# A convolution over 2x2 pixel blocks, attention products issued in halves, and a new order of work, in a fused convolution, attention and expert kernel

## The chip, the cores and the metric

The kernel runs on one core of a Trainium2 chip. The time is that of the device, in microseconds (us), as a median of runs; one further execution was taken with the hardware profiler. A core has a tensor engine (PE; PEld is its loading of weights), a vector engine (DVE), a scalar engine (ACT), GpSimd (POOL), SP, which here only issues transfers, and 16 DMA engines. Each works through its own list of instructions in order and waits on semaphores. Results of PE land in PSUM, eight banks of 512 float32 columns.

## The reference

The input x is float32, 32 batches of 128 channels and 32x32 pixels. Per batch:

```python
xn   = layernorm over channels(x)                    # weights ln_w, ln_b
bcdt = w_bcdt (64x128) @ xn                          # 64 channels
bcdt = conv3x3(bcdt, w_gw, 32 groups of 2 channels, padding 1)
BC, dt = first 32 channels, last 32 channels         # 1024 pixels each
AB   = softmax(dt + A, over pixels) * BC
h    = x @ AB.T                                      # 128 x 32
x    = w_out @ (h @ BC) + x
```

Then, over the 1024 tokens (pixels) of a batch, with t the token rows: one attention layer on the normalised rows (q, k of 64 channels, v of 128, all with a leaky relu, softmax over 1024 keys, residual, layernorm with gamma and beta), added to t. Last, an expert layer over all 32768 tokens: a gate picks one of 8 experts, each token takes the next place of its expert in the order of tokens up to a capacity of 5120, the expert's two matrices (128 to 512 with relu, 512 to 128) are applied, the result is scaled by the gate's probability and added. The output has the layout of x.

## The kernel before, in words

Two programs follow each other. `token_program` (lines 68 to 1259) does everything up to the gate and scatters the normalised-row data of each token into its expert's slots in DRAM, and the token rows themselves (`tokens`) as well. `finish_program` (from line 1263) runs the experts over 71 blocks of 512 slots, scatters the results into `tokens`, and turns finished batches back to channels by pixels.

The work of a batch is cut into named steps ("x_turn", "xs", "bcdt", "bT_turn", "conv", "dt", "dt_exp", "cd_turn", "h", "hh", "g", "y", "ts", "u1n", "u1_turn", "qk", "qk_lrelu", "qk_high", "qk_low", "v", "mask", "mx", "negmax", "mrow", "st", "pv", "ln2s", "ln2n", "ln2m", "ln2g", "t1b", "rowid", "ln3s", "u2_turn", "gate", "gate_turn", "pos", "scatter"). Each engine has a function `one(st, ...)` with its own part of a step, and all engines walk the same list of steps, written out by hand: `head` (line 243), then `steps` (line 222) 20 times, one pass for each new batch, then `tail`. A pass works on five batches at once: its entries carry an offset, so that the convolution of batch c+2, the scores of c+1 and c and the gate of c-1 stand interleaved. An engine that is ready early waits for the semaphore of its step; nothing is reordered at run time.

What the change touches, by step:

- x: SP loads a batch with one transfer (line 439), 4 KB for each channel, issued at "x_turn" of the batch before; "x_turn" on PE transposes it in eight pieces to pixels by channels (even pixels, then odd, line 1098), ACT copies all 1024 columns (two banks, `work`) at once.
- "bcdt": eight products of 64 columns; DVE multiplies by 1/std; "bT_turn" transposes so that the 128 partitions hold 64 channels at even columns and 64 at odd columns of the image; ACT adds a bias and writes the padded image `img` (lines 708, 710).
- "conv" (line 1128): six products of 512 columns, for two column shifts and three rows, into one bank. "dt": DVE takes the maximum over 512 pixels (line 890), exchanges it between the two pixel halves, forms the shift of the exponential (lines 892 to 898); ACT copies BC and exponentiates dt (lines 716, 719).
- "cd_turn": one small product sums exp(dt) over the pixel halves (line 1135), four transposes. "h": eight products of 32 columns of weights, summing into four column groups. "hh" (line 1149): one product with `ident2` that adds the four groups. "g" (1154): with w_out; DVE scales by the softmax's sum (916). "y" (1159): eight products of 128 columns, over 32 rows each, in two banks; DVE adds x (921).
- attention: "mx" (1085) computes the scores for the maxima, DVE reduces them (858); "negmax" and "mrow" turn four rows of maxima, and SP copies them into the last row of `qhi` (489); "st" (1194, 1196) computes the scores again as two products, the second with that row, and ACT exponentiates to `pT`. "pv" (1222): for each of 8 groups of 128 queries, eight products of 129 columns, which alternate between two banks; DVE divides and adds (971, 973).
- "t1b" (GpSimd, line 620) fills the token rows of the next stage once the scatter of two batches before has landed; DVE's sum of "y" waits for the "t1b" of the batch before.
- "pos" (1249 to 1254): eleven small bfloat16 products that count, for each token, the earlier tokens of its expert.
- expert stage: `turn_out` (1594) transposes finished rows and `evict` (1403) writes them to every second column of the output tile, even pixels and odd pixels in turn.

## Time and profile before

| | us |
|---|---|
| median of 3 runs | 2141.65 (2141.04 to 2142.93) |
| profiled execution, its own time | 2142.42 |
| its span, first to last instruction | 2140.7 |
| busy in it: PE, PEld | 2003.1, 1642.3 |
| busy in it: DVE, ACT, POOL | 1753.5, 1192.6, 1023.7 |
| token stage, last PE work of it | about 1570 |
| expert stage, first PE work of it | 1590.87 |

A group of the profile is a set of like instructions; "busy" is the time in which at least one of them ran, so with overlapping instructions count times mean is more than busy. A float32 matmul of the program shows as two instructions. An idle time is put down to whatever ended it.

### The profile page before, as it was taken

The numbers are of one execution on the slowest core, as the hardware profiler recorded it, in microseconds if no ns is written. First come the engines' busy times: TensorE is split into PE (matmuls) and PEld (weight loads), VectorE is DVE, ScalarE is ACT, GpSimd is POOL, SyncE is SP. The second block draws the span as 40 slices with busy tenths as digits, with TensorE's granted clock in tenths as the row PEclk, the third lists the DMA queues.
The fourth block names the chain that finished last, engine by engine and source line by source line (L and its number), as shares of the span: only waits on it lengthen the run. The fifth ranks groups of instructions, "written<-read, shape, count | busy, mean of one in ns | idle before, by whom it ended". The sixth has DMA issues, their size and how long they took to land. (4 is left out here: it accounts for less than half of the span.)

```text
span 2140.7 us, 41957 instructions
## 1 busy us (share of the span) xinstructions
PE 2003.1 (94%) x13855; PEld 1642.3 (77%) x13855; DVE 1753.5 (82%) x5467; ACT 1192.6 (56%) x2216; POOL 1023.7 (48%) x1243
## 2 busy tenths in 40 slices
PE   5889999999999999999999999999829999999996
PEld 3567777787778787778787777787629999898985
DVE  3568888888888888888888888888739999898985
ACT  2344555555555555555545555545327777777773
POOL 5112544444544444544444544354436765555654
PEclk7799999999999999999999999999959999999997
DMA  4541323222312111212111212111136778788874
GB/s 179 193 151 35 93 67 95 70 66 60 88 53 70 51 51 52 77 53 70 51 51 55 75 52 69 49 41 47 44 108 197 205 227 268 251 261 261 253 244 174
DMA packets 163512, 243.98 MB, mean 114 GB/s; under 512 B 31039, under 2 KB 110478, under 8 KB 163296
## 3 DMA queue, kind: packets, MB, share of 16 engines
q1 hardware_dynamic: 139856, 187.16, 29.5%
q0 software_dynamic: 17280, 31.84, 4.6%
q10 hardware_dynamic: 6160, 22.30, 2.6%
q8 instruction: 111, 1.82, 0.4%
q14 instruction: 105, 0.86, 0.1%
HBM read 115.95 MB, written 95.56 MB: 99 GB/s over the span
## 5 line engine op out<-in xcount | busy, mean ns | idle before, releaser
L1222 PE MATMUL pvp<-va,pT 128*128 128x129 f32 x4096 | 505.3, 276 | 0.2 <-ACT pT L747 0.2
L1222 PEld LDWEIGHTS pvp<-va,pT 128*128 128x128 f32 x4096 | 485.5, 191 | 22.2 <-issue 12.4
L1393 POOL DMA_INDIRECT token_rows<-res x284 | 313.0, 1102 | 221.2 <-DVE res L1526 148.3
L858 DVE TENSOR_REDUCE mxs<-mxp 128x1 f32<-128x512 f32 x512 | 338.6, 680 | 23.7 <-PE mxp L1085 17.9
L747 ACT ACTIVATE pT<-stp 128x512 f32<-128x512 f32 x512 | 288.5, 597 | 105.8 <-PE stp L1196 101.1
L639 POOL DMA_INDIRECT expert_slots<-rows,slot_i x256 | 284.7, 1112 | 100.7 <-issue 89.3
L1579 PEld LDWEIGHTS e_yp<-w2s,hid 128*128 128x128 f32 x2272 | 294.1, 192 | 19.8 <-ACT hid L1456 0.3
L1579 PE MATMUL e_yp<-w2s,hid 128*128 128x128 f32 x2272 | 299.8, 275 | 0.0
L1456 ACT ACTIVATE hid<-e_hp,b1c 128x512 f32<-128x512 f32 x284 | 195.1, 687 | 112.9 <-PE e_hp L1571 104.9
L1194 PE MATMUL stp<-qhl,klh 128*128 128x512 f32 x512 | 238.7, 466 | 1.3 <-ACT pT L747 0.8
L1085 PE MATMUL mxp<-khi,qhi 127*128 127x512 f32 x512 | 220.5, 459 | 11.7 <-issue 6.4
L1196 PE MATMUL stp<-qhi,khi 128*128 128x512 f32 x512 | 203.4, 397 | 0.0
L1128 PE MATMUL work<-img,wtap 128*128 128x512 f32 x384 | 174.4, 604 | 2.5 <-ACT img L710 2.5
L708 ACT ACTIVATE img<-work,cbias 64x512 f32<-64x512 f32 x32 | 21.8, 682 | 229.2 <-PE work L1119 229.2
L1569 PE MATMUL e_hp<-e_up,w1p 128*128 128x512 f32 x284 | 136.3, 480 | 2.4 <-DVE e_up L1499 2.4
L679 ACT ACTIVATE u<-t,shift_t,rstd_t 128x128 f32<-128x128 f32 x256 | 105.1, 482 | 59.0 <-POOL shift_t L591 59.0
L679 ACT ACTIVATE o<-o,shift,rstd 128x128 f32<-128x128 f32 x256 | 105.2, 483 | 57.1 <-POOL shift L591 56.4
L1128 PEld LDWEIGHTS work<-img,wtap 128*128 128x128 f32 x384 | 71.8, 194 | 83.1 <-issue 81.2
L1427 ACT ACTIVATE e_u<-e_rows 128x128 f32<-128x128 f32 x284 | 123.4, 485 | 21.6 <-DMA e_rows<-expert_slots 21.6
L1085 PEld LDWEIGHTS mxp<-khi,qhi 127*128 127x128 f32 x512 | 93.5, 192 | 51.3 <-DVE mxs L858 30.1
L586 POOL TENSOR_SCALAR var_x<-mv_x 128x8 f32<-128x8 f32 x32 | 8.0, 250 | 242.3 <-DVE mv_x L851 242.3
L1194 PEld LDWEIGHTS stp<-qhl,klh 128*128 128x128 f32 x512 | 97.6, 191 | 32.0 <-issue 16.0
(242 smaller groups left out, 3919.8 us busy)
## 6 DMA issues: line engine op xcount, KB each, us to landing
w1p<-w_parts SPq DMA_DIRECT2D x71, 512.0 KB
expert_slots<-fill ACTq DMA_DIRECT2D x32, 660.0 KB, 4.2
e_rows<-expert_slots SPq DMA_DIRECT2D x71, 264.0 KB, 3.2
w2s<-in_w SPq DMA_DIRECT2D x71, 256.0 KB
xs<-in_x SPq DMA_DIRECT2D x32, 512.0 KB, 5.0
token_rows<-rows SPq DMA_DIRECT2D x32, 512.0 KB, 3.8
f_rows<-token_rows SPq DMA_DIRECT2D x32, 512.0 KB, 6.5
out<-f_cols SPq DMA_DIRECT2D x32, 512.0 KB, 7.3
```

What stands on the lines that cost most here:

```text
L639: g.indirect_dma_start(out=slots, out_offset=bass.IndirectOffsetOnAxis(ap=slot_i[k][:, t:t + 1], axis=0), in_=rows[k][:, t, :], in_offset= ...
L679: last = a.activation(dst[:, t, :], src[:, t, 0:C], ACT.Identity, bias=shift_[:, t:t + 1], scale=rstd_[:, t:t + 1])
L747: a.activation(pT[j][:, kt, :], stp[kt % 2][:], ACT.Exp).then_inc(s["exp_ready"], 1)
L858: v.reduce_max(mxs[:, qt, n % 2:n % 2 + 1], mxp[n % 2][:], AX).then_inc(s["mx_read"], 1)
L1085: mm(mxp[n % 2][:], qhi[k][0:TOP, qt * P:(qt + 1) * P], khi[k][0:TOP, (n % 2) * HALF:(n % 2 + 1) * HALF], start=True, stop=True).then_inc( ...
L1128: last = mm(work[:, 0, :], wtap[:, d, kh, :], img[:, kh:kh + H, d:d + W // 2], start=(d == 0 and kh == 0), stop=(d == 1 and kh == 2))
L1194: mm(stp[kt % 2][:], klh[k][:, kt * P:(kt + 1) * P], qhl[k][:, c * HALF:(c + 1) * HALF], start=True, stop=False)
L1196: mm(stp[kt % 2][:], khi[k][:, kt * P:(kt + 1) * P], qhi[k][:, c * HALF:(c + 1) * HALF], start=False, stop=True).then_inc(s["st_done"], 1)
L1222: last = mm(pvp[qt % 2][:, 0:VA], pT[c][:, kt, n * P:(n + 1) * P], va[k][:, kt, :], start=(kt == 0), stop=(kt == NT - 1))
L1393: g.indirect_dma_start(out=tokens, out_offset=bass.IndirectOffsetOnAxis(ap=res[n % 2][:, q, TOKEN:TOKEN + 1].bitcast(I32), axis=0), in_=re ...
L1456: a.activation(hid[f][:], hp[f][:], ACT.Relu, bias=b1c[n % WBUF][:, f:f + 1], scale=1.0)\
L1579: last = mm(yp[n % 2][:, q, :], hid[f][:, q * P:(q + 1) * P], w2s[n % WBUF][:, f, :], start=(f == 0 and q == 0), stop=(f == FC - 1), skip_ ...
```

## The change

- Pixels of a batch are split in two ways, by row parity and by column parity. x is loaded by row parity: two transfers for each batch, each of every second image row (32 pixels, 128 bytes). Token order follows: a group of 128 tokens holds one row parity and one column parity, and the products of "pos" and the output writes are rearranged for it.
- The 64 channels of bcdt stand as two halves of 32 (BC and dt). The 128 partitions of the image hold 4 pixel positions of a 2x2 block by 32 channels of one half. The convolution is eight products of 256 columns: for each half, four block shifts.
- The bias of the layernorm is no longer added to the image: the image's border is set to its negative once, and the convolution of the bias is added at the copies of BC and dt.
- "dt" exchanges its maxima over four groups of partitions, two exchanges instead of one. "hh" is one product with `same_s` (128 columns), "g" has 128 columns of weights; its scaling moves from DVE to ACT, as four instructions. "y" is four products of 256 columns over 64 rows.
- ACT's and DVE's evictions of the two banks of `work` (x, u1, qk, u2, v) are done bank by bank, each when its bank is ready.
- "pv" is split: "pv_first" issues the first four of its eight products, "pv" the other four and the rest.
- `steps`, `head` and `tail` have a new order. The first batch's waits and constants change with it.

```diff
-        steps = [(("mrow", 1), 0), ("t1b", 0), ("mask", 1), ("conv", 2), ("qk_high", 1), ("qk_low", 1),
-                 (("ln2n", 3), -1), ("dt", 2), ("dt_exp", 2), (("st", 1, 0), 0), (("st", 1, 1), 0), ("ln2m", -1),
...
-                 (("st", 1, 7), 0), ("y", 2), (("pv", 1, 0), 0), (("mrow", 0), 1), ("ts", 2), ("u2_turn", -1),
-                 (("pv", 1, 1), 0), ("gate", -1), ("ln3s", -1), (("pv", 1, 2), 0), (("u1n", 0), 2), (("u1n", 1), 2),
-                 (("u1n", 2), 2), (("mx", 1, 0), 1), (("pv", 1, 3), 0), (("st", 0, 0), 1), (("u1n", 3), 2),
...
-                 ("pos", -1), (("mx", 1, 5), 1), ("v", 2), (("pv", 0, 0), 1), (("mx", 1, 6), 1), ("bcdt", 3),
-                 ("ln2s", 0), (("mx", 1, 7), 1), (("negmax", 1), 1), ("scatter", -1), (("pv", 0, 1), 1),
...
+        steps = [("t1b", 0), ("qk_lrelu", 1), (("pv", 0, 2), 0), (("mrow", 1), 0), ("mask", 1), ("qk_high", 1),
+                 ("ln2m", -1), ("conv", 2), (("pv_first", 0, 3), 0), ("dt", 2), (("st", 1, 0), 0), ("dt_exp", 2),
+                 (("mx", 0, 0), 1), ("ln2g", -1), (("st", 1, 1), 0), (("mx", 0, 1), 1), (("st", 1, 2), 0),
...
+                 ("qk_low", 1), (("pv", 0, 3), 0), (("mx", 0, 6), 1), (("mx", 0, 7), 1), (("st", 1, 7), 0), ("y", 2),
+                 (("negmax", 0), 1), ("ln3s", -1), (("pv_first", 1, 0), 0), (("pv_first", 1, 1), 0), (("mrow", 0), 1),
+                 ("u2_turn", -1), (("pv", 1, 0), 0), ("ts", 2), (("pv", 1, 1), 0), ("gate", -1), ("x_turn", 3),
+                 (("st", 0, 0), 1), ("gate_turn", -1), (("pv_first", 1, 2), 0), (("st", 0, 1), 1), (("st", 0, 2), 1),
...
+                 ("u1_turn", 2), (("st", 0, 6), 1), ("xs", 3), ("scatter", -1), (("st", 0, 7), 1), (("mx", 1, 3), 1),
...
-                sp.dma_start(xs[k][:], x[bass.ds(b, 1)].rearrange("o c n -> (o c) n")).then_inc(x_loaded[k], 16)
+                for r in range(2):
+                    sp.dma_start(xs[k][:, r * HALF:(r + 1) * HALF].rearrange("c (m w) -> c m w", w=W),
+                                 x[bass.ds(b, 1)].rearrange("o c (m r w) -> (o c) r m w", r=2, w=W)[:, r]).then_inc(x_loaded[k], 16)
...
-                    a.activation(img[0:U, 1:H + 1, 0:W // 2], work[0:U, 1, :].rearrange("p (h w) -> p h w", h=H),
-                                 ACT.Identity, bias=cbias[0:U, :], scale=1.0)
-                    a.activation(img[U:P, 1:H + 1, 1:WP], work[U:P, 1, :].rearrange("p (h w) -> p h w", h=H),
-                                 ACT.Identity, bias=cbias[U:P, :], scale=1.0).then_inc(s["img_ready"], 1)
+                    im = work[:, 1, :].rearrange("p (a r q) -> p a r q", a=2, q=W // 2)
+                    for e in range(2):
+                        for r in range(2):
+                            own = slice((2 * e + r) * S, (2 * e + r + 1) * S)
+                            last = a.copy(img[own, :, r:r + H // 2, e:e + W // 2], im[own])
+                    last.then_inc(s["img_ready"], 1)
...
+                if st == "g":
+                    act.wait_ge(s["g_done"], b + 1)
+                    act.wait_ge(s["dt_sumr"], b + 1)
...
+                    for g in range(Q4):
+                        own = slice(g * S, (g + 1) * S)
+                        last = a.activation(gs[own, g % 2, :], work[own, 0, 0:C], ACT.Identity, scale=dtr[own, :])
+                    last.then_inc(s["g_ready"], 1)
...
-                    v.reduce_max(dts[U:P, 0:1], work[U:P, 0, :], AX).then_inc(s["dt_small"], 1)
+                    v.reduce_max(dts[:, 0:1], work[:, 1, 0:NQ], AX).then_inc(s["dt_small"], 1)
...
+                    v.tensor_tensor(dts[:, 2:3], dts[:, 0:1], dts[:, 1:2], ALU.max).then_inc(s["dt_small"], 1)
+                    dve.wait_ge(s["dt_small"], b * 6 + 3)
+                    for g in range(Q4):
+                        last = v.tensor_copy(dts[g * S:(g + 1) * S, 3:4], dts[(g ^ 1) * S:((g ^ 1) + 1) * S, 2:3])
...
-                    for d in range(2):
-                        for kh in range(3):
-                            last = mm(work[:, 0, :], wtap[:, d, kh, :], img[:, kh:kh + H, d:d + W // 2],
-                                      start=(d == 0 and kh == 0), stop=(d == 1 and kh == 2))
+                    for h in range(2):
+                        for d in range(4):
+                            dr, dq = d // 2, d % 2
+                            last = mm(work[:, h, 0:NQ], wtap[:, h, d, :], img[:, h, dr:dr + H // 2, dq:dq + W // 2],
+                                      start=(d == 0), stop=(d == 3))
...
-                        pe.wait_ge(s["state_ready"], 1)
+                        pe.wait_ge(s["mask_ready"], 1)
...
-                    mm(work[:, 0, 128:128 + 2 * S], hT[:], ident2[:], start=True, stop=True).then_inc(s["h_done"], 1)
+                    mm(work[:, 0, P:2 * P], hT[:], same_s[:], start=True, stop=True).then_inc(s["h_done"], 1)
...
-                    for jj in range(Q4):
+                    for j in range(2):
                         for e in range(2):
-                            last = mm(work[:, e, jj * P:(jj + 1) * P], cd[e * S:(e + 1) * S, jj * P:(jj + 1) * P],
-                                      gs[e * S:(e + 1) * S, :], start=True, stop=True)
+                            last = mm(work[:, e, j * 2 * P:(j + 1) * 2 * P], cd[e * U:(e + 1) * U, 0, j * P:(j + 1) * P],
+                                      gs[e * U:(e + 1) * U, :, :].rearrange("p r c -> p (r c)"), start=True, stop=True)
...
+                if isinstance(st, tuple) and st[0] == "pv_first":
...
+                    for kt in range(NT // 2):
+                        mm(pvp[qt % 2][:, 0:VA], pT[c][:, kt, n * P:(n + 1) * P], va[k][:, kt, :],
+                           start=(kt == 0), stop=False)
...
-            copy(cols[b % 2][:].rearrange("c (m e) -> c e m", e=2)[:, e, :], bank(x)[:])\
+            copy(cols[b % 2][:].rearrange("c (m p q e) -> c e p m q", p=2, q=W // 2, e=2)[:, e],
+                 bank(x)[:].rearrange("c (p m q) -> c p m q", p=2, q=W // 2))\
```

## Rows read from the trace of the kernel before

**Rows 1.** The page, parts 1 and 2: busy us (share), and PE's granted clock.
```profile
PE 2003.1 (94%) x13855; PEld 1642.3 (77%) x13855; DVE 1753.5 (82%) x5467; ACT 1192.6 (56%) x2216; POOL 1023.7 (48%) x1243
...
PEclk7799999999999999999999999999959999999997
```
**Rows 2.** Windows: us, each engine's busy (instructions), clock, DMA share, GB/s.
```profile
600.00:1400.00 800.00, 788.40 (x5558) 627.32 (x5558) 686.32 (x2476) 433.46 (x803) 370.34 (x487) 1.00 0.21 58
...
1640.00:1800.00 160.00, 159.65 (x1138) 147.15 (x1138) 148.25 (x280) 124.72 (x234) 103.47 (x93) 1.00 0.75 228
```
**Rows 3.** Timeline of PE in the loop: start, us, instruction.
```profile
1001.76 0.33 PE L1149 MATMUL work<-ident,hT 128*128 128x64 f32 x2
...
1004.75 1.16 PE L1159 MATMUL work<-gs,cd 32*128 32x128 f32 x16
...
1024.54 0.23 PE L1249 MATMUL pvp<-oh_bf,before_bf 128*128 128x64 bf16 x2
...
1024.84 0.48 PE L1085 MATMUL mxp<-khi,qhi 127*128 127x512 f32 x1
...
1035.31 5.32 PE L1128 MATMUL work<-img,wtap 128*128 128x512 f32 x12
...
1040.69 0.39 PE L1196 MATMUL stp<-qhi,khi 128*128 128x512 f32 x1
...
1047.52 0.33 PE L1149 MATMUL work<-ident,hT 128*128 128x64 f32 x2
```
**Rows 4.** Groups by line and shape, PE, 600 to 1400 us: busy, mean ns, idle before.
```profile
L1128 PE MATMUL work<-img,wtap 128*128 128x512 f32 x204 | 90.4, 592 | 0.0
...
L1159 PE MATMUL work<-gs,cd 32*128 32x128 f32 x272 | 19.7, 283 | 0.0
```
**Rows 5.** Waits, 600 to 1400 us: who waited for whom: us, times, longest.
```profile
DVE t L921 <- POOL rows L620: 15.3, 16, 1.3
PEld mxp L1085 <- DVE mxs L858: 13.3, 50, 0.5
...
PE work L1069 <- DVE t L921: 7.3, 16, 0.8
```
**Rows 6.** Groups by line and shape, DVE and ACT, 600 to 1400 us.
```profile
L890 DVE TENSOR_REDUCE dts<-work 64x1 f32<-64x512 f32 x17 | 11.8, 694 | 29.3 <-PE work L1128 29.3
...
L916 DVE TENSOR_SCALAR gs<-work,dtr 64x128 f32<-64x128 f32 x17 | 5.8, 342 | 2.2
...
L892 DVE COPY dts<-dts 32x1 f32<-32x1 f32 x17 | 2.5, 148 | 0.6
...
L679 ACT ACTIVATE u<-t,shift_t,rstd_t 128x128 f32<-128x128 f32 x144 | 59.1, 482 | 26.6 <-POOL shift_t L591 26.6
...
L710 ACT ACTIVATE img<-work,cbias 64x512 f32<-64x512 f32 x17 | 11.6, 684 | 0.2
...
L725 ACT COPY exT<-work 128x256 f32<-128x256 f32 x17 | 6.3, 372 | 8.3 <-PE work L1137 8.3
```
**Rows 7.** DMA packets from 4 to 6 us, then from 1010 to 1016 us.
```profile
DMA packets 1253, 0.23 MB, mean 117 GB/s; under 512 B 1112, under 2 KB 1240, under 8 KB 1253
...
DMA packets 1193, 1.06 MB, mean 176 GB/s; under 512 B 36, under 2 KB 1064, under 8 KB 1192
```
**Rows 8.** Timeline of the start: start, us, instruction, idle before it.
```profile
6.78 0.87 DVE L817 TENSOR_SCALAR wln<-wbc,lnw_c 128x64 f32<-128x64 f32 x1 [6.78 <-DMA gw_s<-in_gate_w]
...
30.73 0.24 PE L1135 MATMUL work<-dts,pairs 64*64 64x1 f32 x2 [2.54 <-ACT cd L719]
...
31.51 0.10 POOL L581 MEMSET reach<- 128x1 f32 x1
```
**Rows 9.** Timeline in the loop; last, a transfer's size and us to landing.
```profile
1008.96 0.66 SPq L489 DMA_DIRECT2D qhi<-nt  x1
...
1015.61 0.48 PE L1194 MATMUL stp<-qhl,klh 128*128 128x512 f32 x1
...
token_rows<-rows SPq DMA_DIRECT2D x17, 512.0 KB, 3.8
```

More of the change, by code:

```diff
@@ L18 @@
 S = 32
-HP, WP = H + 2, W // 2 + 1
+HB, WB = H // 2 + 1, W // 2 + 1
+NQ = N // 4
 Q4 = 4
@@ L531, in _ @@
             pool.wait_ge(s["early_ready"], 1)
-            chain(g.memset(pairs[:], 0.0))
-            for d in (U - S, U, U + S):
-                chain(g.affine_select(out=pairs[:], in_=pairs[:], pattern=[[-1, U]], compare_op=ALU.not_equal, fill=1.0,
-                                      base=-d, channel_multiplier=1))
             chain(g.memset(fill[:], 0.0))
@@ L748, in one @@
                 if st == "u2_turn":
-                    act.wait_ge(s["u2_turned"], b + 1)
                     if not first:
                         act.wait_ge(s["gate_done"], b)
-                    a.copy(u2T[:], workf).then_inc(s["u2T_ready"], 1)
+                    for h in range(2):
+                        act.wait_ge(s["u2_turned"], b * 2 + (h + 1))
+                        last = a.copy(u2T[:, h * HALF:(h + 1) * HALF], work[:, h, :])
+                    last.then_inc(s["u2T_ready"], 1)
                 if st == "gate":
@@ L1054, in _ @@
             mm(mxp[0][:, 192:192 + E], mean_m[:], gw_s[:], start=True, stop=True)
-            mm(mxp[0][:, 128:129], wbc[:].rearrange("p a u -> p (a u)"), lnb_c[:], start=True, stop=True)\
-                .then_inc(s["wcen_psum"], 1)
+            for h in range(2):
+                last = mm(mxp[0][:, 128 + h:129 + h], wrep[:, h, :, :].rearrange("c a u -> c (a u)"), lnb_c[:], start=True, stop=True)
+            last.then_inc(s["wcen_psum"], 1)
             def taps():
@@ L1132, in one @@
                     if first:
-                        pe.wait_ge(s["state_ready"], 1)
+                        pe.wait_ge(s["mask_ready"], 1)
                     wait_apart(pe, s["cd_exp"], b + 1, passed["pe"])
-                    mm(work[0:U, 0, 256:257], pairs[U:P, :], dts[U:P, 4:5], start=True, stop=True).then_inc(s["dt_sum"], 1)
-                    for jj in range(Q4):
-                        last = nc.tensor.transpose(work[:, 1, jj * P:(jj + 1) * P], cd[:, jj * P:(jj + 1) * P], ident[:])
+                    mm(work[:, 0, 256:257], same_s[:], dts[:, 4:5], start=True, stop=True).then_inc(s["dt_sum"], 1)
+                    for n in range(4):
+                        last = nc.tensor.transpose(work[:, 1, n * P:(n + 1) * P], cd[:, n // 2, n % 2 * P:(n % 2 + 1) * P], ident[:])
                     last.then_inc(s["cd_turned"], 1)
@@ L1169, in one @@
                     for h in range(2):
-                        last = mm(work[:, h, :], wqk_s[:], u1T[:, h * HALF:(h + 1) * HALF], start=True, stop=True)
-                    last.then_inc(s["qk_done"], 1)
+                        mm(work[:, h, :], wqk_s[:], u1T[:, h * HALF:(h + 1) * HALF], start=True, stop=True).then_inc(s["qk_done"], 1)
                 if st == "mask":
@@ L1257, in one @@
+                    for g in range(Q4):
+                        mm(pg[:, 1:3], ones_bf[:], oht[:, :, g:g + 1, :].to_broadcast([P, 2, Q4, E]),
+                           start=False, stop=False, skip_group_check=True)
+                    for g in range(Q4):
+                        last = mm(pg[:, 2], ones_bf[:], oht[:, 0, g:g + 1, :].to_broadcast([P, Q4, E]),
+                                  start=False, stop=(g == Q4 - 1), skip_group_check=True)
                     last.then_inc(s["pos_done"], 1)
```

333 lines of the change are left out of this document (196 added, 137 removed), and 331 rows, old and new, of tables (head, steps, tail).

## The prediction

> **What bounds the kernel now.** I read the page's first two parts first: TensorE (PE) is busy 94% of the span, and the granted clock is full except at the start, at one dip and at the end [rows 1]. The busy time by stage then shows two different kernels. In the token stage (600 to 1400 us) PE is busy 788.40 of 800 us and VectorE (DVE) 686.32, with the DMA engines at 21%; in the expert stage (from 1640) PE is busy 159.65 of 160 [rows 2]. The change touches the token stage and, in the expert stage, only the order in which finished rows are turned and written. So its worth is read in the token stage.
>
> One pass of the token loop can be timed by one matmul that occurs once in it: the product "hh" starts at 1001.76 and again at 1047.52, so a pass is 45.76 us [rows 3]. There are 32 batches; I treat each as costing one pass, head and tail included. PE is idle 11.6 us in these 800, 0.66 a pass. With so little idle, matmul time that goes is time that goes, as long as VectorE (39.3 us of work a pass) and the waits don't take its place.
>
> **The change, part by part.**
>
> *The convolution.* Before, six matmuls of 512 columns, each run by the chip as two instructions: 204 instructions in 17 passes, 90.4 us [rows 4], 5.32 us a pass. The timeline agrees: started at 1035.31, and the second half of the next score pair, which can't start before the first has streamed, at 1040.69 [rows 3]; 5.1 to 5.3 us. After, eight matmuls of 256 columns: 16 instructions instead of 12, with half the columns each. By columns that is 4096 against 6144, 2/3, or 3.55 us: -1.77. Bounds: if an instruction had a price of its own beside its columns, the gain shrinks; with all of the price fixed it would be 16/12 x 5.32 = 7.09, +1.77. What speaks against that end is the y row: instructions of 128 columns cost 19.7/272 = 0.07 us each [rows 4], far below 0.44, so the price goes with the columns. I take -1.7; from -1.8 to -1.3.
>
> *y.* Sixteen instructions with 128 columns, two row groups of 32, 1.16 us [rows 3]. After: eight with 256 columns, two row groups of 64, into the same two banks. If neighbours overlap as now, the same; if the pairs stop overlapping, eight times the 0.22 us of a 256-column instruction (0.443/2) is 1.8, +0.6. I take 0; -0.2 to +0.6.
>
> *hh, g and the sum over dt* use 128 instead of 64 columns or rows: no row has these shapes; from nothing to twice the y instruction's 0.07 each, six instructions: 0 to +0.4; I take +0.15. *The placing product (pos)* goes from 11 instructions to 15: from 1024.54 to 1024.84 is 0.30 us for 11 [rows 3], so +0.1 (0 to +0.2).
>
> Matmul time in sum: -1.7 + 0 + 0.15 + 0.1 = -1.45 a pass, 32 times: **-46 us**.
>
> *The stall at the turning of u2.* The waits show one chain that ends on PE: VectorE's sum t waits for GpSimd's rows (15.3 us in 16 waits), which waits for the scatter's DMA, and then PE waits for t, 7.3 us in 16 waits [rows 5]. In the new list the scatter stands 21 entries before the next "t1b" instead of 9, so the rows are there in time. What is late next is "y" itself, whose sum needs its matmuls and g's longer scaling before them. 0.42 us a pass in about 26 passes: **-11 us** (0 to -15, or a new stall of any size, below).
>
> *VectorE.* The maximum over dt reads 256 columns instead of 512: of 694 ns about half, -0.35. The scaling of g leaves for ScalarE, -0.34. Five more instructions of one column at about 150 ns are added in the dt chain, +0.75, one larger copy +0.07, the split of vz +0.15 [rows 6]. Net +0.3: 39.6 us in a pass of 44. Its idle time falls from 6.4 to 4.7 a pass. PE's weight loads for the maximum products already wait for it 13.3 us in 17 passes [rows 5], 0.76 a pass; if that grows as the idle time shrinks, by 6.4/4.7, it is +0.27, in 27 passes about **+7 us** (0 to +20).
>
> *ScalarE (ACT)*, 433.46 us in 17.5 passes [rows 2]. Two image writes of 684 ns become four of the same length, +1.0 (or four of the plain copy); g's scaling becomes four instructions between 372 and 482 ns, +1.7; halved evictions cost about 0.15 each, four times; cd and exp are halved, -0.4 [rows 6]. About +2.9 on 24.8 us a pass: 28 of 44. It is not the bound, but g's step has become 1.7 us where it was 0.34, and the image 2.4 for 1.37. In the loop other products lie between in the list and hide that; in the first and the last batch nothing does: +2.3 each, less 0.5 for each halved eviction: **+3 us**. That cover gone in the loop would cost up to 2.3 a pass.
>
> *Loads of x.* One transfer of 128 long runs becomes two that pick every second image row, 128 bytes a run: 4096 packets. Around 4 to 6 us the queues moved 1253 mostly short packets in 2 us; from 1010 to 1016 they moved 1193, mostly of 512 bytes, in 6 us, not always busy [rows 7]. So 6.5 us from the nearer row, at most 20.6. In the loop this lies beside a pass of 44 us, and in the list the next transfer on SP's queue ("mrow" of the other half) comes half a pass later, some 22 us, so it costs nothing; with that cover gone, up to 20 us a pass. At the start it is exposed: the first weights, queued behind x, end VectorE's idle 6.78 us [rows 8]. I take +3 us (0 to +14).
> The Trainium skill, DMA: Bandwidth & Descriptors, section Specifications, asks for at least 512 B a transfer for line rate; the two rows agree only in that the short packets moved fewer bytes (0.23 MB in 2 us against 1.06 in 6), and by it alone the load would be slower in each batch, still hidden, and the sum unchanged but for the start.
>
> *Constants.* The first "cd_turn" now waits for the last of GpSimd's constants, which ended at 31.6, with two masks more some 32.3; before, its first matmul ran at 30.73 [rows 8]. So it is 1.5 us later, and the first batch's convolution saves nothing (+1.7): **+3 us**, beside the +3 of x.
>
> *Evictions in the expert stage, products in two halves.* The same instructions with other strides, and the same 16 matmuls with others between: 0. The first half of a product cannot start before the same waits as the whole, so splitting only gives PE something to do while a bank is being freed; that is in the stall term.
>
> **Sum**, against the profiled execution's own 2142.42 us (2140.7 of span and 1.7 around it): -46 - 11 + 7 + 3 + 3 + 3 = -41, so 2101; the median of the runs shown is 0.8 lower than that execution, so I forecast **2100 us**, 1.9% faster.
>
> **Rivals.**
> *A, the new row of maxima arrives late (slower).* Of the first half, today the transfer is issued at 1008.96 and the score product that needs it starts at 1015.61, 6.6 us later [rows 9]. In the new list there lie between "mrow" and that product only the turn of u2, two half products, the gate and the turn of x: 8 x 0.11 + 2 x 0.9 + 0.6 + 0.9 = 4.2 us after the transpose, some 3 after the issue. And the stores of token rows (3.8 us to landing [rows 9]) and of the low parts now stand ahead of it in the same queue, where they stood behind it. If the transfer needs 3.8 us as the store does and starts after it, the product waits 0.8 to 4.6 us a pass. At the middle, 2.7 us in 27 passes, it is +73: 2173. It decides from 41/27 = 1.5 us a pass. For it: the order of the list. Against it: the store is ready once t2 is, half a pass earlier; only the low parts hold SP back, and about 5 us of matmuls lie between them and "mrow".
> *B, the new order removes more.* A pass has more in it than its columns: PE's idle, the wait on VectorE and gaps at changes of shape. If another 0.8 a pass goes, -25: 2075. For it: the halves and the evictions by bank shorten each hand-over. Against: only 0.66 a pass is idle.
> *C, half of the gain is eaten*: y without overlap (+0.6 a pass) or VectorE as the new bound near 45 us: +20, so 2120.
> The Trainium skill, TensorEngine Tiling (Array Packing), section Key Properties, says that a change of tiling mode drains TensorE; y goes from four row tiles' mode to two's, h keeps its own, so the number of changes stays, and no row here prices one.
> *D, it does not do what it says*: if a matmul instruction of 256 columns cost what one of 512 does, +1.77 instead of -1.7 a pass, +110, 2210. The y row speaks against it.
>
> **How the numbers follow.** Forecast 0.50 (2085 to 2112), B 0.15 (2060 to 2085), C 0.19 (2112 to 2138), A 0.14 (of which 0.03 near no change), D 0.02. Range 2065 to 2140: it leaves out half of B's lower tail, and A and D, about 0.2. A measurement of this kernel tells about 0.2% from no change, 4.3 us. Faster 0.84, same 0.03, slower 0.13.
>
> **What would show it.** The convolution at about 213 ns of busy time for each of 16 instructions; a pass of 44.2 us between two hh; no wait of PE for t; VectorE near 90% in the loop; the first weights landed at about 10 instead of 6.8 us; expert stage from its first row to its last unchanged. Wrong: score products of the first half waiting at the head of PE for the maxima's transfer; a pass above 45; y at 1.8 us.

## The result, and the profile after

The changed kernel takes 2055.49 us (median of 4 runs, 2051.71 to 2057.47) against 2142.17 (2141.04 to 2142.93) of the kernel before on the same chip: ratio 0.9594, 95% interval 0.9577 to 0.9610. That is 86.7 us faster. The forecast was 2100 with a range from 2065; the time lies below the range, and below the band of the fastest rival, B (2060 to 2085). Its profiled execution took 2056.32 us, with a span of 2054.6.

The page of the changed kernel, parts 1 and 2, and its window over the loop (columns as in [rows 1, 2]):

```profile
PE 1934.3 (94%) x13873; PEld 1669.8 (81%) x13873; DVE 1744.1 (85%) x5637; ACT 1274.3 (62%) x2550; POOL 1042.5 (51%) x1242
...
PEclk8799999999999999999999999999779999999997
```
```profile
600.00:1400.00 800.00, 794.34 (x5885) 676.48 (x5884) 723.88 (x2715) 504.32 (x1036) 414.33 (x519) 1.00 0.27 62
```

PE's share of the span is 94% as before: that number says nothing of the gain. What moved is PEld, from 627.32 to 676.48 us of 800 [rows 2], and VectorE, from 686.32 to 723.88. More work fits in a stretch, since a pass became shorter: of weight loads a pass has 36.4 us, where it had 35.9. The timeline of PE in the loop answers [rows 3]:

```profile
993.02 0.42 PE L1226 MATMUL work<-same_s,hT 128*128 128x128 f32 x2
...
1010.15 0.23 PE L1337 MATMUL pvp<-oh_bf,before_bf 128*128 128x64 bf16 x2
...
1010.56 0.48 PE L1271 MATMUL stp<-qhl,klh 128*128 128x512 f32 x1
...
1025.85 3.73 PE L1205 MATMUL work<-img,wtap 128*128 128x256 f32 x16
...
1035.89 0.46 PE L1226 MATMUL work<-same_s,hT 128*128 128x128 f32 x2
...
1039.03 1.13 PE L1236 MATMUL work<-gs,cd 64*128 64x256 f32 x8
```

From hh to hh it is 42.87 us, where it was 45.76. Over the whole kernel, by the starts of the hh products: the first came at 39.9 us (34.0 before, +5.9); from the first to the last, 31 passes, it is 1344.9 us (1429.7, -84.8); from the last to the first product of the expert stage 121.1 (127.2, -6.1); from there to the end 548.7 (549.8, -1.1). In sum -86.1, the difference of the spans.

The groups of the loop that answer to [rows 4, 6] (busy, mean ns | idle before):

```profile
L1205 PE MATMUL work<-img,wtap 128*128 128x256 f32 x288 | 66.9, 384 | 0.0
L1236 PE MATMUL work<-gs,cd 64*128 64x256 f32 x152 | 21.6, 402 | 0.2 <-ACT gs L781 0.2
L757 ACT COPY img<-work 32x512 f32<-32x512 f32 x72 | 41.7, 579 | 103.0 <-PE work L1190 102.4
L781 ACT ACTIVATE gs<-work,dtr 32x128 f32<-32x128 f32 x76 | 27.0, 355 | 2.9 <-PE work L1231 2.1
L959 DVE COPY dts<-dts 32x1 f32<-32x1 f32 x76 | 11.0, 145 | 1.4
L946 DVE TENSOR_REDUCE dts<-work 128x1 f32<-128x256 f32 x19 | 8.0, 423 | 4.6 <-PE work L1205 4.6
```

The convolution is 66.9/288 = 232 ns an instruction, 3.7 us a pass instead of 5.3 (forecast: 213 ns and 3.55). y is 21.6/19 = 1.14 us, as before (1.16). So these two terms of the forecast hold, -1.6 and 0; they are 1.6 of the 2.9 us that a pass lost.

### The profile page after: what moved, and what is told of

The parts are those of the page before. It is cut to its first block and busy times, and to the rows that moved or that the text cites. A ratio compares the mean times of both kernels' runs of the same rounds, so it can differ in the third digit from the quotient of the medians.

```text
span 2054.6 us, 42527 instructions
## 1 busy us (share of the span) xinstructions
PE 1934.3 (94%) x13873; PEld 1669.8 (81%) x13873; DVE 1744.1 (85%) x5637; ACT 1274.3 (62%) x2550; POOL 1042.5 (51%) x1242
## 5 line engine op out<-in xcount | busy, mean ns | idle before, releaser
L675 POOL DMA_INDIRECT expert_slots<-rows,slot_i x256 | 325.8, 1273 | 99.6 <-issue 91.9
L1299 PEld LDWEIGHTS pvp<-va,pT 128*128 128x128 f32 x2048 | 251.5, 191 | 28.2 <-issue 15.6
L1299 PE MATMUL pvp<-va,pT 128*128 128x129 f32 x2048 | 264.2, 276 | 0.1
L1305 PE MATMUL pvp<-va,pT 128*128 128x129 f32 x2048 | 262.7, 274 | 0.0
L1305 PEld LDWEIGHTS pvp<-va,pT 128*128 128x128 f32 x2048 | 249.9, 191 | 7.4 <-issue 1.6
L1271 PE MATMUL stp<-qhl,klh 128*128 128x512 f32 x512 | 224.1, 438 | 5.4 <-DMA qhi<-nt 4.2
L1155 PE MATMUL mxp<-khi,qhi 127*128 127x512 f32 x512 | 211.0, 437 | 5.7 <-DVE mxs L914 3.5
L757 ACT COPY img<-work 32x512 f32<-32x512 f32 x128 | 74.1, 579 | 168.8 <-PE work L1190 167.6
L1205 PE MATMUL work<-img,wtap 128*128 128x256 f32 x512 | 124.1, 397 | 0.0
L623 POOL TENSOR_SCALAR var<-mv_t 128x8 f32<-128x8 f32 x32 | 6.2, 193 | 231.5 <-DVE mv_t L907 231.4
L1205 PEld LDWEIGHTS work<-img,wtap 128*128 128x128 f32 x512 | 98.6, 197 | 20.3 <-ACT img L757 6.5
```

Of the source, the lines that this page charges most:

```text
L675: g.indirect_dma_start(out=slots, out_offset=bass.IndirectOffsetOnAxis(ap=slot_i[k][:, t:t + 1], axis=0), in_=rows[k][:, t, :], in_offset= ...
L1155: mm(mxp[n % 2][:], qhi[k][0:TOP, qt * P:(qt + 1) * P], khi[k][0:TOP, (n % 2) * HALF:(n % 2 + 1) * HALF], start=True, stop=True).then_inc( ...
L1205: last = mm(work[:, h, 0:NQ], wtap[:, h, d, :], img[:, h, dr:dr + H // 2, dq:dq + W // 2], start=(d == 0), stop=(d == 3))
L1271: mm(stp[kt % 2][:], klh[k][:, kt * P:(kt + 1) * P], qhl[k][:, c * HALF:(c + 1) * HALF], start=True, stop=False)
L1299: mm(pvp[qt % 2][:, 0:VA], pT[c][:, kt, n * P:(n + 1) * P], va[k][:, kt, :], start=(kt == 0), stop=False)
L1305: last = mm(pvp[qt % 2][:, 0:VA], pT[c][:, kt, n * P:(n + 1) * P], va[k][:, kt, :], start=False, stop=(kt == NT - 1))
```

## The experiments

Three parts of the change were put in and taken out alone: A, the convolution with all that belongs to it; E, the evictions of `work` bank by bank (x, u1, qk, u2, v); O, the new lists with the split pv. "Pass" is the time between the hh products of the 6th and the 26th batch, over 20; PE idle is 800 less PE's busy time in the window of 600 to 1400 us, times pass/800. Both come from the one profiled execution, which can differ from the median: that of O, E took 2106.05 us, that of E 2144.59, that of O, A 2084.03. In all seventeen profiles the expert stage, in which at most the order of the output's writes differs, took between 549 and 556 us from its first product to the end; differences of a few us in the time are within that.

| kernel | time | ratio, 95% | pass | PE idle a pass |
|---|---|---|---|---|
| before | 2142 | 1 | 45.79 | 0.66 |
| E | 2136.7 | 0.9961 to 0.9984 | 45.81 | 0.72 |
| A | 2134.4 | 0.9943 to 0.9973 | 45.11 | 1.62 |
| A, E | 2136.4 | 0.9966 to 0.9985 | 45.09 | 1.62 |
| O | 2127.0 | 0.9920 to 0.9956 | 45.38 | 0.50 |
| O, E | 2096.4 | 0.9765 to 0.9798 | 44.67 | 0.18 |
| O, A | 2078.1 | 0.9677 to 0.9723 | 43.80 | 0.57 |
| O, A, E (the change) | 2055.5 | 0.9577 to 0.9610 | 43.00 | 0.30 |

**The old order with the new work (A, E).** The changed kernel, with the `steps`, `head` and `tail` of before, each pv directly behind its pv_first:

```diff
-        steps = [("t1b", 0), ("qk_lrelu", 1), (("pv", 0, 2), 0), (("mrow", 1), 0), ("mask", 1), ("qk_high", 1),
+        steps = [(("mrow", 1), 0), ("t1b", 0), ("mask", 1), ("conv", 2), ("qk_high", 1), ("qk_low", 1),
...
```

> The changed kernel with the order of the kernel before: steps, head and tail are the old lists, each pv directly behind its pv_first. Theory T1 (two separate gains: arithmetic about 45 us by the shorter convolution, order about 40 us by taking short waits out of PE's list): 2095 to 2105, pass 44.3 us. Rival T2 (the arithmetic and the evictions by bank give all, the order nothing): 2050 to 2062, pass 42.9. Rival T3 (the old order does not fit the new work, which has later g and image steps): 2120 or more.

Measured: 2136.44. Of the three only T3 allows this; 5.6 us are left of 86.7.

**The new order alone (O).** The lists and the two steps of pv, put into the kernel before:

```diff
-                    for kt in range(NT):
+                    for kt in range(NT // 2):
                         mm(pvp[qt % 2][:, 0:VA], pT[c][:, kt, n * P:(n + 1) * P], va[k][:, kt, :],
...
```

> The kernel before with only the new lists and the split pv; convolution, loads, evictions are those of before. T1 (additive): 2095 to 2105, pass 44.3 us. T2: 2138 to 2146, pass 45.7. T3 (the new order helps only with the new work): 2142 or more. A sum of the gains of this and of the old-order kernel near 86 us speaks for T1.

Measured: 2127.01, between the ranges. The two gains sum to 21 us, not 86: T1 falls, and with it the way in which I had added terms. T2 falls by the run before this one: the new work without the order gave 5.6 us. Of T3 half is left: the order alone gives something, but most of it comes only beside the rest. PE's waits show what the new list, in this kernel, has opened (PEld is the wait of a weight load, during which the matmuls before it can still count as busy; L1138 are here the products of bcdt, L1195 those of qk):

```profile
PEld work L1138 <- issue: 10.2, 18, 0.6
...
PEld work L1195 <- ACT u1T L755: 6.8, 18, 0.4
...
PE work L1138 <- DVE vz L984: 5.2, 18, 0.3
```

Before the change neither wait for an eviction is there. The products of bcdt wait until v's eviction has freed `work`, those of qk until u1 is copied.

**Evictions over both banks in the changed kernel (O, A).**

```diff
-                    for h in range(2):
-                        act.wait_ge(s["x_turned"], b * 2 + (h + 1))
-                        last = a.copy(xT[:, h * Q4:(h + 1) * Q4, :].rearrange("p t c -> p (t c)"), work[:, h, :])
+                    act.wait_ge(s["x_turned"], b * 2 + 2)
+                    last = a.copy(xT[:].rearrange("p t c -> p (t c)"), workf)
...
```

> The changed kernel, but the copies of x, u1, qk, u2 and v read both banks in one instruction, as before the change; one wait for the second bank. If the evictions by bank are worth nothing by themselves (forecast at no cost and no gain): within 4 us of the changed kernel, about 2055. If each of the five hand-overs lets PE or the consumer start 0.3 to 0.5 us earlier on the path: 0.8 us a pass or more is lost, 2080 or later. If the added instructions only loaded ACT and VectorE: a few us faster, 2045 to 2052.

Measured: 2078.14, just under the 2080 that was set for hand-overs on the path, and 0.80 us a pass lost, as set for it. The forecast had put them at a small load on ACT.

**pv in one piece.** The changed kernel, each of the eight pv_first directly before its pv:

```diff
-                 ("qk", 2), (("pv_first", 0, 0), 1), (("pv_first", 0, 1), 1), ("v", 2), (("pv", 0, 0), 1),
+                 ("qk", 2), ("v", 2), (("pv_first", 0, 0), 1), (("pv", 0, 0), 1),
...
```

> The changed kernel with each product pv issued in one piece, its first half moved back to directly before its second half; the rest of the new order stays. If the halves fill the times in which PE waits (exp of the last key tile, a freed bank): 0.4 to 1.0 us a pass is lost, 2068 to 2087. If splitting is worth nothing, as the prediction had it: 2051 to 2060.

Measured: 2173.85 (ratio 1.0131 to 1.0179), a pass of 47.09, more than expected and slower than before the change. PE's waits, 600 to 1400 us (us, times, longest):

```profile
PE mxp L1264 <- DVE nmx L897: 23.7, 17, 1.4
PE work L1238 <- ACT qka L775: 14.8, 17, 0.9
PE work L1191 <- ACT cd L747: 13.6, 16, 0.9
PE work L1169 <- DVE bT L916: 8.4, 17, 0.5
```

60.5 us in 17 passes, 3.6 a pass. So the halves are not small change: the new list counts on one or two of them behind each of four hand-overs (negmax to mrow, qk to v, conv to cd_turn, bT to its turning).

**The new convolution alone, in the old order (A).** The two edits of (A, E) and (O, A) together: old lists, and evictions over both banks:

```diff
-                    for h in range(2):
-                        act.wait_ge(s["u1_turned"], b * 2 + (h + 1))
...
+                    act.wait_ge(s["u1_turned"], b * 2 + 2)
+                    last = a.copy(u1T[:], workf)
...
```

> The changed kernel with the old order (each pv directly behind its pv_first) and with the copies of x, u1, qk, u2 and v over both banks at once: of the change only the convolution over 2x2 blocks and what belongs to it (loads, dt, hh, g on ACT, y, pos). The old order with the evictions by bank took 2136. Theory T4 (the old list has hand-overs, above all the image's four copies and g's four scalings on ACT, that have no cover in it, so PE waits where it multiplied before): the evictions by bank shorten such hand-overs too, so without them 2140 to 2160. Rival T5 (the evictions by bank only load the queues in the old order): 2125 to 2136. Rival of my prediction's own (46 us for the matmuls in any order): 2096.

Measured: 2134.42. T4's range was too high, and by the time alone T5 fits; but the evictions by bank, added to this, bring nothing either (2136.4, overlapping intervals). The profile shows where the convolution's gain stays. PE's waits:

```profile
PE mxp L1123 <- issue: 7.9, 17, 1.4
PE work L1173 <- ACT img L731: 7.8, 18, 0.4
PE work L1204 <- ACT gs L755: 5.5, 17, 0.5
PE work L1106 <- ACT xT L705: 4.2, 17, 0.3
```

PE is busy 771.21 of 800 us, so 1.64 us less a pass than before, and idle 0.96 more. From the first to the last hh this profile is 13.5 us shorter than that of before, and its first hh comes 4.3 us later. Three of the four waits are for ACT; the image's four copies (2.35 us) and g's four scalings (1.46) now stand where the old list has no cover for them. The fourth, the first score product for the maxima, waits for ACT too in one of its cases (khi, 0.4 us); for the others the profile names no releaser.

**The new order with the evictions by bank and the old convolution (O, E).** To O is added, for each of the five:

```diff
-                    act.wait_ge(s["x_turned"], b + 1)
...
-                    a.copy(xT[:].rearrange("p t c -> p (t c)"), workf).then_inc(s["xT_ready"], 1)
+                    for h in range(2):
+                        act.wait_ge(s["x_turned"], b * 2 + (h + 1))
+                        last = a.copy(xT[:, h * Q4:(h + 1) * Q4, :].rearrange("p t c -> p (t c)"), work[:, h, :])
...
```

> The kernel before with the new lists, the split pv and the evictions by bank, but the old convolution. The new order alone took 2127. If the evictions by bank are worth in it what they are in the changed kernel (23 us): 2104, and the rest to the changed kernel's 2055 is the arithmetic, 49 us against my 46. If they are worth it only beside the new arithmetic: 2120 to 2128.

Measured: 2096.4, where 2104 was expected. From here to the changed kernel it is 41 us, the arithmetic's term (forecast: 46). From before to here it is 46 us without a single matmul less (forecast: 11); the profiled execution, the longest of the five, shows 36 of them. Its window, and its two groups of score products beside those of before and of O alone:

```profile
600.00:1400.00 800.00, 796.72 (x5658) 641.68 (x5657) 696.38 (x2521) 447.97 (x882) 405.13 (x499) 1.00 0.23 60
...
L1232 PE MATMUL stp<-qhl,klh 128*128 128x512 f32 x282 | 122.9, 436 | 0.0
L1123 PE MATMUL mxp<-khi,qhi 127*128 127x512 f32 x286 | 117.3, 432 | 0.4 <-issue 0.4
```
```profile
L1194 PE MATMUL stp<-qhl,klh 128*128 128x512 f32 x280 | 130.8, 467 | 0.0
L1085 PE MATMUL mxp<-khi,qhi 127*128 127x512 f32 x280 | 120.6, 456 | 0.5 <-issue 0.4
```
```profile
L1219 PE MATMUL stp<-qhl,klh 128*128 128x512 f32 x279 | 121.3, 435 | 0.1
L1110 PE MATMUL mxp<-khi,qhi 127*128 127x512 f32 x279 | 113.9, 429 | 0.4 <-issue 0.4
```

The pass lost 1.12 us, but only 0.48 of it was idle time of PE. It is tempting to find the rest in the means, 467 and 456 ns before, 436 and 432 here. But O alone has these shorter means too (435, 429), with a pass that lost only 0.41. They follow the neighbour in the list: a score product lasts 0.40 us behind another one, 0.48 behind most others, and 0.79 behind the convolution or qk, where two of the 16 first halves (L1194) of a pass stood before the change and none stands now. Here the first stands behind the convolution, the last behind a score product:

```profile
1040.06 0.79 PE L1194 MATMUL stp<-qhl,klh 128*128 128x512 f32 x1
1040.69 0.39 PE L1196 MATMUL stp<-qhi,khi 128*128 128x512 f32 x1
1040.92 0.40 PE L1194 MATMUL stp<-qhl,klh 128*128 128x512 f32 x1
```

What does show the gain is the time from each start of a matmul on PE to the next, with nothing counted as busy or idle. Added up by the step that the later one belongs to, over the passes from the 6th to the 26th hh, in us a pass:

| step | before | E | A | O | O, E | O, A | the change |
|---|---|---|---|---|---|---|---|
| turning of u2, behind t | 1.50 | 1.51 | 0.98 | 0.87 | 0.87 | 0.88 | 0.87 |
| bcdt, behind v's eviction in the new list | 2.07 | 2.09 | 2.04 | 2.55 | 2.05 | 2.55 | 2.03 |
| qk, behind u1's copy in the new list | 1.52 | 1.52 | 1.52 | 1.73 | 1.53 | 1.78 | 1.52 |

The new list takes away the stall behind t (0.63 us a pass, where PE's idle time there was 0.42) and opens two others, 0.48 and 0.21. (In A, in the old list, the stall behind t shrinks too.) The evictions by bank close just these two: 0.50 and 0.20 of the 0.71 us a pass from O to O, E, and 0.52 and 0.26 of the 0.80 from O, A to the change. In the old list the two are not there, so E finds nothing in its loop. Of the five evictions the trace thus names v and u1 as the ones that count; they were not tested one by one.

**Evictions by bank alone (E).** The same edit in the kernel before.

> The kernel before with nothing but the evictions by bank. Each bank is copied when its four matmuls are done, so a consumer starts some 0.5 us earlier, at the price of 0.15 us of ACT or VectorE for each. If PE waited anywhere for such a hand-over in the old order (xT 1.4 us and t 7.3 us of 800): 2125 to 2138. If not: 2140 to 2144. If the price counts: above 2144.

Measured: 2136.68, inside the first range. The profile can't say where the 5 us come from: its execution took 2144.59, the longest of the seven (the others 2135.60 to 2139.67). In it the pass is unchanged (45.81), and so is PE's wait for t (7.4 us, 16 times).

**Two of the eight halves moved back.** In the changed kernel:

```diff
-                 (("negmax", 0), 1), ("ln3s", -1), (("pv_first", 1, 0), 0), (("pv_first", 1, 1), 0), (("mrow", 0), 1),
-                 ("u2_turn", -1), (("pv", 1, 0), 0), ("ts", 2), (("pv", 1, 1), 0), ("gate", -1), ("x_turn", 3),
+                 (("negmax", 0), 1), ("ln3s", -1), (("mrow", 0), 1),
+                 ("u2_turn", -1), (("pv_first", 1, 0), 0), (("pv", 1, 0), 0), ("ts", 2), (("pv_first", 1, 1), 0), (("pv", 1, 1), 0), ("gate", -1), ("x_turn", 3),
...
```

> The changed kernel with only two of the eight half products moved back: pv_first of groups 4 and 5, which stand between negmax and mrow, again directly before their pv. With all eight moved back, PE waited 23.7 us in 17 passes for nmx (1.4 us each), and the time was 2174. Theory T6 (a half product is cover for one definite hand-over, here VectorE's maxima, and its price is that wait): 0.9 to 1.4 us in 27 passes, 2079 to 2093, and the trace shows PE waiting for nmx. Rival T7 (the loss of 118 us is not in single places but in the sum of all): less than a quarter of the 118, under 2070.

Measured: 2103.1 (0.9792 to 0.9829), a pass of 44.75. T6 holds in kind, and its price was too low. One wait is new in PE's list:

```profile
PE mxp L1280 <- DVE nmx L913: 27.6, 16, 2.4
```

1.7 us each, and the pass grew by 1.75: what PE waits there, the kernel pays in full.

**g's scaling on VectorE, in the old order with A.** ACT's step g goes, and VectorE gets:

```diff
+                if st == "g":
+                    dve.wait_ge(s["g_done"], b + 1)
...
+                    for g in range(Q4):
+                        own = slice(g * S, (g + 1) * S)
+                        last = v.tensor_scalar(gs[own, g % 2, :], work[own, 0, 0:C], dtr[own, :], None, ALU.mult)
```

> The kernel with only the new convolution in the old order, and the scaling of g back on VectorE (four instructions there instead of four on ACT). In the old order a pass of 45.1 us held 1.6 us of PE idle, of which 0.3 before y, ended by ACT's g scaling, 0.44 before conv (ACT's image copies), 0.25 at xT and 0.46 at the first mx. Theory T4 (the old list has no cover for the longer steps on ACT): PE's wait before y goes, the others stay; 0.3 a pass, 2123 to 2130 against 2134. Rival T8 (the waits are the room left by one loop through all passes, so that closing one opens another): 2131 to 2138, PE idle unchanged.

Measured: 2195.06 (1.0229 to 1.0265). Both theories miss, by some 60 us. PE's wait before y did go, but t and the maxima, which VectorE makes behind g, became late:

```profile
PE work L1106 <- DVE t L955: 17.8, 17, 1.7
PE mxp L1253 <- DVE nmx L879: 17.3, 15, 1.4
```

These two are 2.1 us a pass. Some 15 of the 60 us, by my estimate, are another matter: in ten of the 29 passes from the third on the granted clock of PE falls from its full level (2.4 GHz) to half (1.2 GHz) for 3.4 us, and in the middle of the loop such a pass takes 48.5 to 48.8 us, where most others take about 47.0. In A the clock does so in one of the 29.

**The same in the changed kernel.**

> The changed kernel with g's scaling back on VectorE. VectorE is busy 724 of 800 us there and ACT 504. If VectorE's time is what the pass of 43.0 us hangs on: four instructions of some 0.3 us, up to 1.2 us a pass more, 2065 to 2090. If hand-overs count and not loads: g comes sooner, PE's weight load for y waited 7.0 us in 19 passes for ACT's g; same or up to 10 faster, 2045 to 2058.

Measured: 2094.8 (0.9753 to 0.9792), a pass of 44.37, slightly above the first range. The timeline shows the chain (VectorE, and the last line PE):

```profile
1018.69 1.42 DVE L978 TENSOR_SCALAR gs<-work,dtr 32x128 f32<-32x128 f32 x4
1020.14 1.23 DVE L1021 TENSOR_TENSOR qkl<-qk,qkh 128x1024 fp32r<-128x1024 f32 x1
...
1023.07 1.22 DVE L985 TENSOR_TENSOR t<-work,xT 128x1024 f32<-128x1024 f32 x1
1024.20 0.15 DVE L909 TENSOR_REDUCE nmx<-mxs 128x4 f32<-128x8 f32 x1
...
1024.40 0.27 PE L1285 MATMUL mxp<-ident,nmx 128*4 128x128 f32 x1 [1.12 <-DVE nmx L909]
```

1.42 us on VectorE ahead of nmx, 1.12 us of waiting on PE, 1.37 us more a pass. Having g's four scalings on ACT and not on VectorE was worth some 38 us; the forecast had booked the move as 0.34 us of relief inside a load.

**The start, and the changed kernel again.** First weights on ACT's queue, and the image's wait of the first batch behind the bias's 16 matmuls:

```diff
-                    pe.wait_ge(s["img_ready"], b + 1)
                     if first:
...
                         last.then_inc(s["conv_bias"], 1)
+                    pe.wait_ge(s["img_ready"], b + 1)
```

> The changed kernel with the first five weights on ACT's queue, ahead of its own loads, so that they do not stand behind the two transfers of x; and with the 16 matmuls of the bias's convolution ahead of the first batch's wait for the image. First weights at about 6 us instead of 8.39, and the bias matmuls (3.5 us) beside ACT's image copies: the first convolution starts at some 21 to 23 instead of 25.98, so 3 to 5 us less in all, 2050 to 2053, ratio 0.0015 to 0.0025 under that of the changed kernel. Rival: the start is hidden, since later batches' loads or the expert stage take it back: no difference.

> The changed kernel itself, on the same chip as the three others, as their base: 2055, ratio 0.959 to 0.961.

Measured: 2056.07 (0.9587 to 0.9628) and, for the changed kernel, 2056.90 (0.9585 to 0.9615). The first convolution starts at 23.37 instead of 25.98 and the first hh 1.7 us earlier; the medians don't tell the two apart. Inconclusive.

**Three copies moved off VectorE.** nt, kt and hT are copied by ACT:

```diff
-                    v.tensor_copy(nt[j][:], mxp[0][0:Q4, 0:P]).then_inc(s["nt_ready"], 1)
...
+                    a.copy(nt[j][:], mxp[0][0:Q4, 0:P]).then_inc(s["nt_ready"], 1)
```

> The changed kernel with three copies out of PSUM moved from VectorE to ACT: the turned maxima (nt, two a pass), the turned mask (kt) and h (hT). On VectorE they are 0.25 to 0.28 us each, 1.05 us of a pass of 43.0 in which VectorE is busy 38.9. With g's four scalings added to VectorE (1.42 us) the pass grew by 1.37. Theory T9 (VectorE's list is as tight as PE's, and its work on the way to the maxima is paid one for one): a pass of 42.0 to 42.4, 2025 to 2040, and VectorE about 88%. Rival T10 (one-sided: more on VectorE costs, less gives nothing, since PE's own matmuls and their hand-overs then end last): 42.8 to 43.0, 2050 to 2057. Rival T11 (ACT takes nt late, behind its exponentials): slower than 2060.

> The same, with the change to the start as well (first weights on ACT's queue, the bias's convolution ahead of the image's wait), the version meant to be the fastest. In the profile of that change alone the first hh was 1.7 us earlier and the first product of the expert stage 3.0 us; its median did not tell it from the changed kernel. Here 0 to 4 us under the time of the kernel with the three copies moved.

Measured: 2059.85 (0.9601 to 0.9633), and with the start as well 2066.77 (0.9608 to 0.9657), where 0 to 4 us less than the first was expected. In the profile of the second the expert stage took 556.4 us, of the first 548.8, and the passes are the same (42.90 and 42.92): nearly all of its loss is where nothing was edited. The window of the first, and a wait in it:

```profile
600.00:1400.00 800.00, 791.41 (x5851) 676.06 (x5850) 709.06 (x2618) 515.80 (x1098) 405.01 (x512) 1.00 0.26 61
```
```profile
PE stp L1271 <- DMA qhi<-nt: 4.8, 3, 3.7
```

VectorE is down to 88.6%, and the pass is 42.92 against 43.00. T9 falls. T10's pass holds, its time is missed by 3 us. T11 has a share in that: PE's wait for the transfer of the row of maxima is 4.8 us in 800 instead of 1.2, and from the first to the last hh this profile is 4.4 us longer than that of the changed kernel, lost in the 28th to the 30th. So less on VectorE gave nothing in the steady passes; whether it would give something in the others without more on ACT was not tested. Neither beats the changed kernel.

**x loaded twice**, the second time into a tile that nobody reads:

```diff
+                    sp.dma_start(xtwo[k][:, r * HALF:(r + 1) * HALF].rearrange("c (m w) -> c m w", w=W),
+                                 x[bass.ds(b, 1)].rearrange("o c (m r w) -> (o c) r m w", r=2, w=W)[:, r]).then_inc(x_loaded[k], 16)
```

> The changed kernel, with each transfer of x issued twice, the second into a tile that nobody reads, and x taken as loaded when all four are in. If the loads of 128-byte runs are hidden beside a pass, as the prediction had it (a cost of 0 in the loop, some us at the start): 2056 to 2064. If SP's queue or the transfers' share of the DMA engines already delays the rows of maxima: 0.5 us a pass or more, 2072 and later, with PE waiting for qhi's DMA.

Measured: 2062.64 (0.9605 to 0.9637). The pass is 43.03 with the DMA share at 0.34 instead of 0.27, and PE's wait for qhi's transfer is 1.2 us in 800, as without. Nearly all of the loss is at the start, where the first hh comes at 46.0 instead of 39.9 us. The loads are hidden in the loop, as forecast.

## Why the prediction was wrong

- *Matmul time, -46.* Right in size: 41 us between O with E and the full change, and 1.6 to 1.7 us a pass wherever the new list is used. Of its small terms, pos takes 0.41 us instead of 0.30, as forecast. But it was not free of the order, as my working had it. In the old order the same saving gives 7.5 us (13.5 in the passes from the first to the last hh, where it gives 54.1 from O, E to the change), since the steps that A lengthens on ACT have no cover there. I had named that ("that cover gone in the loop would cost up to 2.3 a pass") and not asked what the new list does for it.
- *The order, -11.* This is the step that failed. I took what order can give back to be one stall, priced at PE's idle time there, 0.42 us a pass. Measured, the order alone gives 15 us, and order and evictions by bank together 46, before any arithmetic changes. Rival B had this mechanism, and I turned it down with "only 0.66 a pass is idle"; its own price, 25 us, was too low as well. That sentence is the error: O, E has a pass 1.12 us shorter with 0.48 less of idle time, so more than half of what was won had counted as busy. Part of it can be named: the stall behind t is 0.63 us from start to start and 0.42 of idle time, and in O the weight loads of qk wait 6.8 us in 800 for u1's copy with no idle time of PE at all. The rest, the stretches of the list in which O gains beside the stall at t, is not traced to single waits. The Trainium skill, Perfetto Trace Analysis, section Identifying the Most-Contended Engine, says that matmul busy share is no good measure of headroom, since matmuls are pipelined, and names the share of weight loads instead, beside the share of peak arithmetic. This trace agrees with the first: PE was busy 98.6% and had room. Its loads were 78.4% before and 84.6% after; how much of the remainder can be had neither number says.
- *Evictions by bank.* For the loop I counted only their fixed price, 0.15 us for each on ACT. They are worth 23 us (O, A to O, A, E) or 31 us (O to O, E) in the new list, since they close two hand-overs that this list opens, and nothing measurable beside A in the old.
- *VectorE, +7.* The share is as forecast, 90.5%, though of a shorter pass: 38.9 us of work, not 39.6. The cost was not: PE's weight loads for the maxima wait 3.6 us for VectorE instead of 13.3 [rows 5], and taking 1.05 us off VectorE gave nothing, with ACT doing that work. What counts is whether VectorE's list brings nmx and t in time.
- *x and constants, +3 and +3.* The first hh is 5.9 us later, near the sum of the two, but by luck: the first weights came at 8.39 us, not 10, the constants didn't bind at all, and 3.54 us of bias matmuls at the start were missing from my sum, as was in these two terms the first batch's share of ACT's +3.
- *Rival A.* PE waited 1.2 us in 800 for the row of maxima's transfer. The price of C's first cause, y without overlap, did not occur: with two row groups of 64 it has the same 1.1 us.
- *Expert stage, 0.* -1.1 us; right, and within what it varies by (551.8 us in the second profile of the changed kernel, 548.7 in the first, 549.8 before). The drain before it was 6.1 us shorter, a term that I didn't have; it goes with the new lists (120.3 in O, 127.8 in A).
- *Loads of x in the loop, 0.* Right. A load of 256 KB in runs of 128 bytes lands in 3.8 us, where one of 512 KB in long runs took 4.9. That is no proof of a lower rate, since other transfers of 256 KB in the changed kernel took 3.2 us (qhl from qkl) and 4.3 (klh from qkh). The engines' time is: loading x twice adds 12 GB/s to 62 and 0.07 to their busy share of 0.27, where the kernel before moved 58 GB/s with 0.21. In this the rule that I had weighed, of the Trainium skill, DMA: Bandwidth & Descriptors, section Specifications, agrees with the traces; in the loop it costs nothing.

What stays open: which of the moves in the lists, beside the two halves tried alone, makes how much of O; which of the five evictions makes how much of E; and where E's 5 us alone come from.

## What to carry to other kernels

An engine with pipelined instructions that is 98% busy may still be waiting: look at the waits of its weight loads, and compare two runs by the time from start to start, step by step, before saying that only the idle share can be won. The mean duration of one form misleads: here it followed the neighbour in the list and not the wait. In a list written by hand, arithmetic, order and hand-overs do not add: here 7, 5 and 15 us alone, 87 together; so a saving is to be priced in the list in which it will run. Before moving an operation between engines, follow what stands behind it on that engine to the next thing that PE waits for: 1.4 us there cost 1.4 us a pass, while 1.0 us moved the other way gave none.

## What the runs showed of the hardware

- Matmul price goes with the columns: the convolution's 256-column float32 instructions were 232 ns of busy time each, its 512-column ones 443 (granted clock 1.00 in both).
- The duration that the profile gives a matmul goes with the one before it: the 512-column score product took 0.40 us behind another score product, 0.48 behind most others, 0.79 behind the 512-column ones of the convolution and of qk.
- At the start the same instructions are slower. The first y took 2.08 us, in a stretch where the granted clock is at its half level (1.2 GHz), and 1.13 in the loop at the full one (2.4 GHz). The first 16 convolution instructions took 6.74 us against 3.73 in the loop; nearly all of that lies before the profile's clock record begins (32 us), so for them the clock is not shown.
- An operation on 32 partitions costs what a larger one does: 579 ns for a copy of 32x512 on ACT and 590 for one of 128x512; 345 ns for g's 32x128 on VectorE (in the run that puts it there) and 342 for 64x128 before.
- Transfers of 128-byte runs raised the packets in the loop's 800 us from 31,049 to 101,392; doubling these loads left the pass at 43.03 us against 43.00.
